# Attention values returned through DRAM in place of TensorE transposes, with new query and key blocks

## The reference

```python
qkv = x @ w_qkv.T * hid ** (-0.5)                 # [16, 1024, 768]
q, k, v = heads of 16 channels, 16 heads
scores = einsum('bhqd,bhkd->bhqk', q, k) * d ** (-0.5)
attn = softmax(scores) * (s / np.sqrt(s - 1.0))
out = einsum('bhqk,bhkd->bhqd', attn, v) * s ** (-0.5)
x = x + out.reshape(b, s, hid) @ w_o.T * hid ** (-0.5)
```

## Time and profile before

| | |
|---|---|
| three runs | 5750.79, 5751.51 (median), 5752.28 us |
| profiled execution, its own time | 5750.62 us |
| its span, first to last instruction | 5748.9 us |
| mean granted TensorE clock | 0.976 |
| busy over the span: PE / DVE / ACT / POOL | 94% / 78% / 62% / 26% |
| `projection_stage` | 1678 to 2003 us of the span |
| `attention_stage` | 2004 to 4799 us, 128 pairs |

### The profile page before, as it was taken

The page is one execution under the profiler, slowest core; times in us unless marked ns, Lnnn a source line. Parts: engine busy times, 40 slices in busy tenths (PEclk is TensorE's granted clock), DMA queues, the critical chain, the costliest instruction groups (busy, mean ns, idle before and its releaser), DMA issues. The chain is left out here.

```text
span 5748.9 us, 131254 instructions
## 1 busy us (share of the span) xinstructions
PE 5428.0 (94%) x50092; PEld 3660.4 (64%) x50092; DVE 4498.2 (78%) x7377; ACT 3566.0 (62%) x5406; POOL 1473.5 (26%) x1948
## 2 busy tenths in 40 slices
PE   7999668999989889999999999999999997799999
PEld 6777457999978734444444444444444444699998
DVE  7888695555557689999999999999999996755554
ACT  5777562333325458888888888888888886433332
POOL 4655453333310000111111111111111114533332
PEclk9999889999999989999999999999999998999999
DMA  2222482222229811121112111111211113222221
GB/s 74 78 84 78 137 259 77 88 93 93 89 96 333 310 56 49 58 60 57 57 59 60 57 56 60 59 57 56 60 58 57 57 54 104 75 89 93 95 86 49
DMA packets 317697, 512.58 MB, mean 89 GB/s; under 512 B 36442, under 2 KB 221156, under 8 KB 311152
## 3 DMA queue, kind: packets, MB, share of 16 engines
q1 hardware_dynamic: 291912, 441.44, 24.2%
q0 software_dynamic: 24576, 64.56, 3.5%
q10 hardware_dynamic: 808, 1.07, 0.1%
HBM read 338.59 MB, written 185.60 MB: 91 GB/s over the span
## 5 line engine op out<-in xcount | busy, mean ns | idle before, releaser
L1773 DVE TENSOR_REDUCE at_best<-at_psM 128x2 f32<-128x1024 f32 x2048 | 2430.7, 1221 | 227.5 <-PE at_psM L1830 214.3
L1729 ACT ACTIVATE at_p<-at_psE 128x1024 f32<-128x1024 f32 (+1 forms) x2688 | 2077.1, 824 | 529.5 <-PE at_psE L1846 515.7
L1846 PE MATMUL at_psE<-at_q,at_k 50*128 50x512 f32 x4096 | 1174.0, 436 | 7.5 <-ACT at_p L1729 6.3
L1830 PE MATMUL at_psM<-at_k,at_q 48*128 48x512 f32 x4096 | 1093.6, 458 | 37.5 <-DMA at_k<-scratch_qk 27.4
L1857 PE MATMUL at_psO<-at_p,at_v 128*17 128x256 f32 x16384 | 1109.9, 383 | 0.1
L1122 ACT ACTIVATE e_h_hi<-e_psH 128x512 fp32r<-128x512 f32 x512 | 306.7, 599 | 916.0 <-PE e_psH L90 864.4
L1846 PEld LDWEIGHTS at_psE<-at_q,at_k 50*128 50x128 f32 x4096 | 548.7, 185 | 462.4 <-issue 223.6
L1196 DVE SCALAR_TENSOR_TENSOR e_h_lo<-e_psH,e_h_hi 128x512 fp32r<-128x512 f32 x512 | 353.9, 691 | 595.9 <-ACT e_h_hi L1122 505.8
L1857 PEld LDWEIGHTS at_psO<-at_p,at_v 128*17 128x17 f32 x16384 | 364.1, 96 | 542.7 <-issue 345.4
L1830 PEld LDWEIGHTS at_psM<-at_k,at_q 48*128 48x128 f32 x4096 | 471.3, 185 | 312.2 <-DVE at_best L1773 147.2
L90 PE MATMUL e_psE<-e_w_hi,e_h_hi 128*128 128x256 f32 x2048 | 583.1, 285 | 0.0
(11 more groups left out here) (213 smaller groups left out, 8456.5 us busy)
## 6 DMA issues: line engine op xcount, KB each, us to landing
e_w_raw<-in_w SPq DMA_DIRECT2D x64, 1024.0 KB
scratch_qk<-cp_qkh SPq DMA_DIRECT2D x64, 512.0 KB
scratch_qk<-cp_qkl SPq DMA_DIRECT2D x64, 512.0 KB
at_q<-scratch_qk SPq DMA_DIRECT2D x256, 128.0 KB
at_k<-scratch_qk SPq DMA_DIRECT2D x252, 128.0 KB
scratch_v<-cp_va SPq DMA_DIRECT2D x32, 544.0 KB
at_v<-scratch_v SPq DMA_DIRECT2D x126, 136.0 KB, 10.0
a_x<-in_x SPq DMA_DIRECT2D x32, 512.0 KB
```

The lines of the kernel that those rows point to most:

```text
L1729: nc.scalar.activation(P[:, u:u + n, :], src, ACT.Exp, scale=HD ** -0.5).then_inc(p_ready, 1)
L1773: nc.vector.reduce_max(best[j % 2][:, h, :, qt], psM[h][:], AX_X).then_inc(m_taken, 1)
L1830: last = nc.tensor.matmul(psM[h][:, a, :], Q[j][r, 128 * qt:128 * qt + 128], K[j][r, 512 * h:512 * h + 512], start=True, stop=True)
L1846: last = nc.tensor.matmul(psE[:, u - u0 if n == 2 else 2, :], K[j][r, 128 * kc:128 * kc + 128], Q[j][r, 512 * half:512 * half + 512], star ...
```

## The change

Nothing is transposed on TensorE any more except the maxima. The values stay with channels on partitions:

1. `turn_values`, `turn_out`, `normalise` and `take_out` go. After `take_values`, SP stores the 128x512 tile `OT` of a pair to a new DRAM scratch `ot` (`store_values`, 256 KB). Per unit (pair pp takes unit pp-4: one half of the channels, 256 queries), SP loads the values (`raw`, 128x256) and, by a DMA that repeats the row of sums for each of the 16 channels of its head, the divisors (`den`, 128x256).
2. DVE inverts the 128x256 tile of divisors (`invert`, after m = 12), POOL multiplies, then splits as before.
3. SP's order: the unit is loaded first in three pairs of four, and behind the store in the fourth; queries and keys of pair pp+3 wait only for the key scores of pair pp-1, values for the last values.
4. The scratch `qk` is [256 heads, 2 halves of the tokens, 4 parts, 16 channels, 512 tokens], so that 32 rows of a head's high and low part form one block and each row is read in two pieces of 2 KB; the projection stores it in eight DMAs of 256 KB a step where there were four of 512 KB.
5. PE's order of queries, keys and values within a pair is new; the maximum is taken before g = 13, not 11.
6. The end of the stage does the last four units with loads, reciprocals and products of their own (`divide_end`).

```diff
-    qkb = qk.rearrange("r (b h) d n -> b r (h d) n", h=H)
+    qkb = qk.rearrange("(b c h) s r d n -> s b c r h d n", c=2, h=H // 2)
...
-                        sp.dma_start(row(qkb, i)[r, :, half].rearrange("(c p) n -> p c n", p=128), buf[s][:, cs, :].bitcast(F32)).then_inc(qkv_stored[s], 16)
+                        for c in range(2):
+                            sp.dma_start(row(qkb[s], i)[c, r], buf[s][:, 2 * part + c, :].bitcast(F32)).then_inc(qkv_stored[s], 16)
...
-    qkp = qk.rearrange("r (u x) d n -> u x r d n", x=2)
+    qkp = qk.rearrange("(u a) s r d n -> u a (r d) s n", a=2)
+    rows = ot.rearrange("(b k i) a (m w) c -> b k m (i a) w c", k=2, i=4, m=4)
...
-        OUT_AT, MAX_AT, VALUES_AT, NORM_AT = 1, 11, 3, 3
+        OUT_AT, MAX_AT, VALUES_AT, INVERT_AT = 1, 13, 3, 12
...
-                eng.dma_start(Q[j][r:r + 32, :].bitcast(F32), row(qkp, pp)[a, 0:2]).then_inc(qk_loaded[j], 16)
+                eng.dma_start(Q[j][r:r + 32, :].bitcast(F32), row(qkp, pp)[a, 0:32]).then_inc(qk_loaded[j], 16)
...
+            def store_values(p):
+                sp.wait_ge(oT_ready, p + 1)
+                sp.dma_start(ot[p].rearrange("a r c -> r a c"), OT[:].rearrange("r (a c) -> r a c", a=2)).then_inc(oT_stored, 16)
+            def load_unit(u, slot, b, k, m, needed):
+                sp.wait_ge(oT_stored, 16 * needed)
+                after(sp, ofT_ready, u - 1)
+                sp.dma_start(raw[slot][:], rows[b, k, m][:, 0:HD, :]).then_inc(unit_loaded[slot], 16)
+                sp.dma_start(den[slot][:], rows[b, k, m][:, HD:HD + 1, :].broadcast_to([8, HD, 256])).then_inc(unit_loaded[slot], 16)
...
+                if pb % 4 > 0:
+                    next_unit()
                 if there(pp + 3):
                     after(sp, e_done, pp * NG)
+                    load_queries(sp, pp + 3, (pb + 3) % 4)
+                    load_keys(sp, pp + 3, (pb + 3) % 4)
                     after(sp, pv_done, pp * KC)
-                    load_pair(pp + 3, (pb + 3) % 4)
+                    load_values(sp, pp + 3, (pb + 3) % 4)
+                if not first(pp):
+                    store_values(pp - 1)
+                if pb % 4 == 0:
+                    next_unit()
...
             def split_out(u, slot, k, m, b):
-                pool.wait_ge(xo_taken, u + 1)
+                pool.wait_ge(rden_ready, u + 1)
+                nc.gpsimd.tensor_tensor(oT[slot][:], raw[slot][:], den[slot][:], ALU.mult).then_inc(ofT_ready, 1)
...
-            def normalise(p, pb, b):
-                dve.wait_ge(t_done, p + 1)
-                nc.vector.reciprocal(rden[:], tv[:, :, :, HD]).then_inc(rden_ready, 1)
-                nc.vector.tensor_tensor(O[:, :, 32 * pb:32 * pb + 32].rearrange("p t (a d) -> p a t d", a=2), tv[:, :, :, 0:HD],
-                                        rden[:].unsqueeze(3).broadcast_to([128, 2, KC, HD]), ALU.mult).then_inc(o_ready, 1)
+            def invert(u, slot):
+                dve.wait_ge(unit_loaded[slot], 32 * (u // 2 + 1))
+                nc.vector.reciprocal(den[slot][:], den[slot][:]).then_inc(rden_ready, 1)
+            def divide_end(m):
+                dve.wait_ge(end_loaded[m], 32)
+                nc.vector.reciprocal(end_den[:, span], end_den[:, span]).then_inc(end_rden_ready, 1)
+                dve.wait_ge(end_rden_ready, m + 1)
+                nc.vector.tensor_tensor(end_raw[:, span], end_raw[:, span], end_den[:, span], ALU.mult).then_inc(end_oT_ready, 1)
...
                 if kc == 0 and heads[0] == 0:
-                    after(pe, o_ready, pp)
+                    after(pe, oT_ready, pp)
...
-                output(), query(0, -1), key(0), last_values(6)
-                query(1, 0), query(2, 0), key(1), key(2), last_values(7)
-                key(3), query(3, 3), key(4)
-                    turn_values(pp - 1)
-                key(5), query(4, 5), query(5, 5), key(6), values(pp, pb % 4, 0)
...
+                output(), query(0, -1), key(0), query(1, 0), last_values(6)
+                query(2, 0), key(1), key(2), last_values(7)
+                key(3), query(3, 3), query(4, 3), key(4), values(pp, pb % 4, 0)
+                key(5), key(6), query(5, 6), values(pp, pb % 4, 1, (0,))
+                key(7), query(6, 7), key(8), values(pp, pb % 4, 1, (1,))
+                query(7, 8), key(9), query(8, 9), key(10), values(pp, pb % 4, 2)
+                key(11), query(9, 11), key(12), query(10, 12), next_max_rows(), values(pp, pb % 4, 3, (0,))
+                query(11, 12), key(13), key(14), values(pp, pb % 4, 3, (1,))
                 values(pp, pb % 4, 4, (0,)), key(15), query(12, 15), key(16), values(pp, pb % 4, 4, (1,))
-                key(17), query(13, 17), query(14, 17), key(18), key(19), values(pp, pb % 4, 5)
+                key(17), query(13, 17), key(18), query(14, 18), key(19), values(pp, pb % 4, 5)
                 key(20), query(15, 20)
```

More of the change, by code:

```diff
@@ L1372, in group @@
             def group(g, s, i):
-                after(act, qkv_stored[s], 80 * i)
+                after(act, qkv_stored[s], 144 * i)
                 for c in range(4):
@@ L1477, in _, with attention_stage @@
             groups(pe, NG, group)
-def attention_stage(nc, T, stage, x, qk, v, woT, out):
+def attention_stage(nc, T, stage, x, qk, v, ot, woT, out):
     N, D = x.shape
@@ L1508, in attention_stage @@
         OT = sb("oT", [128, 512], F32)
-        rden = sb("rden", [128, 2, KC], F32)
-        O = sb("o", [128, KC, D], F32)
+        raw = [sb(f"raw{s}", [128, 256], F32) for s in range(2)]
+        den = [sb(f"den{s}", [128, 256], F32) for s in range(2)]
+        end_raw = sb("end_raw", [128, S], F32)
+        end_den = sb("end_den", [128, S], F32)
         oT = [sb(f"ofT{s}", [128, 256], F32) for s in range(2)]
@@ L1654, in _ @@
             batches(pair)
+            store_values(NP - 1)
+            sp.wait_ge(oT_stored, 16 * NP)
+            for m in range(4):
+                span = slice(256 * m, 256 * m + 256)
+                sp.dma_start(end_den[:, span], rows[B - 1, 1, m][:, HD:HD + 1, :].broadcast_to([8, HD, 256])).then_inc(end_loaded[m], 16)
+                sp.dma_start(end_raw[:, span], rows[B - 1, 1, m][:, 0:HD, :]).then_inc(end_loaded[m], 16)
             store_out(NP - 9, B - 2, PB - 1)
@@ L1732, in take_values @@
                 act.wait_ge(pv_done, KC * p + KC)
-                after(act, t_done, p)
+                after(act, oT_stored, 16 * p)
                 nc.scalar.activation(OT[:], psO[:], ACT.Copy).then_inc(oT_ready, 1)
-            def take_out(u, slot, bank):
-                act.wait_ge(xo_done, u + 1)
-                after(act, xo_lo_ready, u - 1)
-                nc.scalar.activation(oT[slot][:], bank[:, 128:384], ACT.Copy).then_inc(xo_taken, 1)
             def scale_y(u, b, n, bank):
@@ L1756, in pair @@
                         take_max(pp + 1, (pb + 1) % 4)
-                    if g == MAX_AT and has_turned(pp):
-                        take_out(pp - 4, pb % 2, psE[:, 2, :])
                     exps(pp, g)
@@ L1861, in values @@
                     last.then_inc(pv_done, 1)
-            def turn_values(p):
-                pe.wait_ge(oT_ready, p + 1)
-                for c in range(4):
-                    last = nc.tensor.transpose(psO[:, 128 * c:128 * c + 128], OT[:, 128 * c:128 * c + 128], T.ident[:])
-                last.then_inc(t_done, 1)
-            def turn_out(k, m, needed, bank):
-                pe.wait_ge(o_ready, needed)
-                for t in range(2):
-                    last = nc.tensor.transpose(bank[:, 128 + 128 * t:256 + 128 * t], O[:, 2 * m + t, 128 * k:128 * k + 128], T.ident[:])
-                last.then_inc(xo_done, 1)
             def project_out(b, n, bank):
@@ L1951, in _ @@
             project_out(B - 2, PB - 1, psE[:, 0, :])
-            turn_values(NP - 1)
-            pe.wait_ge(m_taken, 16 * NP)
-            for m in range(4):
-                turn_out(1, m, NP, psM[m // 2][:, m % 2, :])
             for n in range(PB):
```

72 lines of the change are left out of this document (37 added, 35 removed).

## The result

Four runs of the kernel before gave a median of 5751.9 us (5750.79 to 5763.5), four of the changed kernel 5964.2 (5954.74 to 5969.47): a ratio of 1.0365, interval 1.0349 to 1.038. The change costs **212 us**. The forecast was 5803, with 5850 as the upper end: the direction was right, the size was not. The profiled execution of the changed kernel took 5965.3 us, its span is 5963.6.

What follows compares the result with a forecast made beforehand. TensorE looked like the bound, VectorE close behind, coupled through two banks. Pairs +52, start -12.5 and end +12 made +51.5 us on the median of 5751.5: 5803 us, range 5765 to 5850.

Steps and rivals of the forecast that it cites:

- The reciprocal: 128x256 reciprocal on VectorE in an attention pair: 6 ns a column, 1.69 us, 1.60 of it on the engine.
- Cheap: Rival: the attention reciprocal takes only 0.33 us on VectorE, like the product; total 5672 us, chance 0.07.
- steep slope: Rival: every column of the attention reciprocal costs 8.75 ns, 2.28 us on the engine; total 5887 us, chance 0.08.
- The ring: Closed attention path: query 12, reduction 12, reciprocal, reduction 13, query 15, TensorE's list round; 21.18 us a pair.
- the list's own part: TensorE's work from query 15 round to the next pair's query 12: 16.93 us, of 20.48 a pair.
- The two added waits: Attention queries 1 and 8 wait for reductions, about 0.4 us each; less 0.2 already held, +0.6 us a pair.
- GpSimd's product: Added multiplication on POOL in the attention stage: POOL is busy 292 of 2450 us, so it fits.
- the term of the pairs: 124 attention pairs with a reciprocal, each 21.75 us, 0.42 above before: +52 us (+15 to +95).
- The rival without added waits: Attention pairs: reciprocal as priced, the two waits not added, 21.05 to 21.1 us; total 5720 us, chance 0.12.
- The start: Attention stage's first loads spread over 16 DMA engines, first matmul at 2011.5: -12.5 us (0 to -15).
- The end: End of the attention stage, with store, loads, reciprocals and products of the last units: +12 us (+8 to +18).
- Unit late: Rival: in fourth attention pairs the store lands behind loads, reciprocal waits 2 us, 31 times; 5865 us, chance 0.05.

Runs made afterwards that it cites:

- e3: Kernel before, each 512 KB projection store cut into two of 256 KB, layout unchanged: 5750.3 us (0.9994).
- e11: Changed kernel, each 256 KB projection store written as 16 blocks of 8 rows instead of 8 blocks of 16: 5826.1 us (1.0122).
- e6: As e5, but the reciprocal covers only the first 16 of 256 columns, so most output is wrong: 5690.6 us (0.9897).
- e10: As e5, with a second reciprocal of the same size, its result never read, in front of the first: 6246.7 us (1.0858).
- e9: As e5, with the reciprocal after reduction 5 in place of 12: 6282.8 us (1.0924).
- e12: As e9, but in each fourth pair the reciprocal stays after reduction 12: 6054.1 us (1.0518).
- e2: Kernel before with only the new blocks of queries and keys, stores and loads: 5892.7 us (1.0235).
- e4: Kernel before, layout and stores unchanged, loads of queries and keys with the 16 channels outermost: 5739.9 us (0.9974).
- e1: Changed kernel with the query and key scratch, its stores and its loads as in the kernel before: 5870.0 us (1.0195).
- e5: e1 with the loads of e4, that is the change without its new layout: 5821.0 us (1.0117).
- e8: As e5, but sums inverted as 128x16, then repeated over channels by a load; reciprocal after reduction 3, or 9 in fourth pairs: 5703.6 us (0.9918).

## Why the prediction was wrong in size and right in sign

**The failed step** is one sentence: "The projection's eight smaller stores lie beside its matmuls: nothing." It holds for what the words name, the count and the size (e3: nothing). It fails for what they leave out. The paragraph before it used the rule of the Trainium skill ("DMA: Bandwidth & Descriptors", section "Why a DMA increments its semaphore by 16 and not by 1") that the slowest dimensions set how many engines a transfer uses, and used it for the loads alone. It also left out that the stage had no room: its DMA engines were busy 0.95. The stores' DRAM side became [8 heads, 16, 512] with a gap between the heads. By the rule that is 8 engines, and the runs agree: 4 to 5 tenths busy and 8 packets in flight with 8 blocks, full with 16 (e11).

The price could have been worked out from the old trace. A step moves 2.10 MB of stores, 0.56 of values and 0.52 of inputs. At half of 385 GB/s the first take 10.9 us, the others at 385 another 2.8: 13.7 us a step against 326.8 / 32 = 10.2, that is +112 us in 32 steps. Measured: 467.0 / 32 = 14.6, +140; the last 28 us are not taken apart (while the values' and inputs' transfers run, 262 to 383 GB/s flow, and the granted clock is 0.88 between TensorE's gaps). No rival held this case, since all five were about the attention stage.

Point by point, the rest:

- **The reciprocal**: 1.69 us forecast, 1.74 measured; 1.60 and 1.66 on the engine. Over 16 to 256 columns it is (1743 - 243) / 240 = 6.25 ns a column, within the 5.5 to 8.75 of the earlier trace rows. "Cheap" and "steep slope" fall. The 8.3 ns a column, an estimate from the repeat count of 8 that the Trainium skill ("VectorE: DVE Perf Modes", section "First, the fixed hardware budget") gives, was a third too high.
- **The ring**: right, and the term that carried the sign. e6 opens it (20.74 us), e10 lengthens it, e9 and e12 move it. The forecast of 20.48 for TensorE alone is 20.74 in e6; only 0.07 us of that pair are gaps (2392 of 2400 us busy), so the list's own part was sized some 0.2 too low. 21.75 was forecast for a pair with the reciprocal; 21.69 is measured in the timeline and 21.78 as the mean.
- **The two added waits**: at query 1 it is there, 0.19 for a forecast 0.4, at query 8 it is not. That the pair came out as summed is in part luck: a list priced some 0.2 too low stands against waits priced too high. The waits of weight loads for reductions rose too, from 112.8 us to 280.4, but which of them lengthen the pair is not settled.
- **GpSimd's product**: "so its added product fits" went by GpSimd's busy time. Its product and splits also stand in a chain behind the reciprocal, and in one pair of eight the output projection waits 1.08 us for them. That is 11 us in all, as much as the term of the pairs (63) lies over its forecast (52).
- **The rival without added waits** has an error in its sum: the prediction's own ring is 21.18, 0.15 under the old 21.33, which makes 19 us and a forecast of 5732; 5720 used 21.05 to 21.1.
- **The start**: -12.5 forecast, -12.6 measured, and shown to be the loads' spread by e2 and e4.
- **The end**: +12 forecast, +14 measured.
- **"Unit late"**: not in the changed kernel; in e1, where the loads stay on few engines, it costs 0.31 us a pair, as its condition said. With the clock that falls behind its waits that is by size all of e1's miss (0.31 x 127 = 39 us, 33 missing).

## What to carry to other kernels

When a layout changes, take both sides of every transfer that touches it, the writers too, and count the blocks of the outermost dimension; then look at the DMA share of the stage that issues them, for in a stage at 0.95 a halved spread reaches the time (4.4 us a step of 10.2 here). Here the spread that the new layout was to bring could be had from the reader's side alone, by the order of dimensions in a load (e4, e5). And an operation whose price goes by columns is to be done on the compact form: 2048 sums as 128x16 cost 0.24 us, repeated first they cost 1.74, and on a ring of two engines that difference was the sign of the result (e8 against e5).

## What had not been expected of the hardware

- A wait of 1.4 us of TensorE once a pair costs more than itself: the granted clock behind it is 0.50 to 0.64 for some 4 us in 69 of 71 cases, and the matmuls there take nearly twice their time (1.91 for 1.06 us). In the changed kernel, with gaps of 0.2 us twice a pair, the stage's mean is 1.00, and of its 15 gaps of 1.08 us only 4 are followed by a lower clock (0.56 to 0.68 over 4 us). This fits e9, e10 and e12, which lie far above what the ring alone gives.
- The same stores with 16 blocks of 8 rows for 8 blocks of 16 move 330 GB/s instead of 218 in the whole mix.
- The reciprocal costs 6.25 ns a column, six times the product's 1 ns.
